# Graph attention layer on one core: node masks and counts made in the edge stage, part of the softmax work given to Pool, the last two adds of x given to DVE

## The reference

```python
h   = relu(layernorm(x))
msg = relu(h[src] + edge_attr);  p = msg @ W_fc.T + b_fc
scores = p @ Q.T                                   # one score for each head
w = exp(scores - segment_max(scores, dst)[dst])
alpha = w / max(segment_sum(w, dst)[dst], 1e-9)
pooled = [segment_sum(alpha[:, h:h+1] * p, dst) for each head]
mean_p = segment_sum(p, dst) / max(deg, 1)
gate = softmax(mean_p @ Wg.T + bg)                 # over the heads
out = x + sigmoid(sum_h gate[:, h] * pooled[h])
```

## Time and profile before

| | us |
|---|---|
| median of three runs (744.27 to 744.82) | 744.5 |
| the profiled execution | 740.5 |
| its span, from first to last instruction | 738.8 |
| DVE busy in the span | 487.2 |
| PE busy in the span | 553.3 |

### The profile page before, as it was taken

The page is one execution under the profiler, slowest core; times in us unless marked ns, Lnnn a source line. Parts: engine busy times, 40 slices in busy tenths (PEclk is TensorE's granted clock), DMA queues, the critical chain, the costliest instruction groups (busy, mean ns, idle before and its releaser), DMA issues.

```text
span 738.8 us, 12420 instructions
## 1 busy us (share of the span) xinstructions
PE 553.3 (75%) x2474; PEld 435.4 (59%) x2475; DVE 487.2 (66%) x1651; ACT 383.7 (52%) x661; POOL 440.3 (60%) x334
## 2 busy tenths in 40 slices
PE   3418988988889867989003998889888778877775
PEld 2206866766668656767002876777666666655554
DVE  4118677868679767878998766666565655554552
ACT  2105455646557455664130244666766575666663
POOL 7765556666651655640000256677878787778887
PEclk9999899989999999999655999999999999999998
DMA  7434455555553577775000799999999999999998
GB/s 222 136 92 145 142 163 172 169 167 171 169 173 117 162 230 254 242 256 188 25 0 3 251 361 366 307 305 324 358 327 340 335 345 316 320 332 343 336 340 277
DMA packets 137238, 171.53 MB, mean 232 GB/s; under 512 B 10096, under 2 KB 123784, under 8 KB 137202
## 3 DMA queue, kind: packets, MB, share of 16 engines
q10 hardware_dynamic: 91344, 90.23, 37.2%
q1 hardware_dynamic: 33010, 42.70, 18.2%
q0 software_dynamic: 12848, 38.20, 16.2%
HBM read 111.50 MB, written 59.60 MB: 232 GB/s over the span
## 4 chain that ended last, share of the span: by engine, by line
PE 46%; DVE 14%; issue 9%; ACT 8%; another core or an unknown queue 7%; POOL 6%; ACTq 4%; DMA 2%; DVEq 2%; POOLq 0%; SPq 0%
PE bank L726 23%; PE bank L809 16%; POOL arena L444 6%; PE bank L716 5%; ACT arena L583 5%; DVE spread L1196 3%; ACTq L586 2%; ACT bank L559 2%; DVE p_keep L997 1%; ACTq L538 1%; DVE stats L977 1%; DVEq L1200 1%; ACTq L591 1%; DMA p_keep<-in_x_dram,idx 1%
## 5 line engine op out<-in xcount | busy, mean ns | idle before, releaser
L809 PE MATMUL bank<-p_keep,spread 128*128 x1172 | 273.4, 387 | 54.4 <-DVE spread L1196 46.1
L444 POOL TENSOR_TENSOR arena<-arena 128x1024 f32<-128x1024 f32 x96 | 224.7, 2350 | 144.0 <-ACT arena L583 143.6
L809 PEld LDWEIGHTS bank<-p_keep,spread 128*128 128x128 f32 x1172 | 217.4, 191 | 111.2 <-issue 84.2
L1196 DVE TENSOR_SCALAR spread<-bank,rel,wgt 128x128 f32<-128x128 f32 x586 | 195.8, 403 | 130.9 <-PE bank L809 78.7
L726 PE MATMUL bank<-w_all,arena 128*128 128x264 f32 (+1 forms) x784 | 232.1, 423 | 43.2 <-ACT arena L491 22.3
L726 PEld LDWEIGHTS bank<-w_all,arena 128*128 128x128 f32 (+1 forms) x784 | 146.1, 207 | 68.7 <-ACT arena L491 36.3
L583 ACT ACTIVATE arena<-bank 128x1024 f32<-128x1024 f32 x97 | 99.2, 1022 | 144.8 <-PE bank L809 131.9
L431 POOL DMA_INDIRECT p_keep<-in_x_dram,idx x124 | 120.4, 971 | 71.6 <-issue 32.6
L491 ACT ACTIVATE arena<-bank 128x256 f32<-128x256 f32 x196 | 72.9, 373 | 103.9 <-remote 51.4
L431 POOL DMA_INDIRECT arena<-in_x_dram,idx x72 | 70.1, 974 | 60.8 <-ACT arena L483 33.9
L559 ACT ACTIVATE bank<-zero 128x1024 f32<-128x1024 f32 x98 | 100.5, 1026 | 3.0
(11 more groups left out here) (197 smaller groups left out, 163.7 us busy)
## 6 DMA issues: line engine op xcount, KB each, us to landing
out_dram<-arena ACTq DMA_DIRECT2D x97, 512.0 KB, 4.5
arena<-in_x_dram ACTq DMA_DIRECT2D x73, 512.0 KB, 5.4
arena<-in_edge_attr_dram SPq DMA_DIRECT2D x48, 512.0 KB
arena<-in_x_dram POOLq DMA_DIRECT2D x24, 512.0 KB, 5.7
p_spill<-p_keep SPq DMA_DIRECT2D x16, 512.0 KB
p_keep<-p_spill SPq DMA_DIRECT2D x16, 512.0 KB, 5.5
p_keep<-in_x_dram,idx POOLq DMA_INDIRECT x124
arena<-in_x_dram,idx POOLq DMA_INDIRECT x72
```

The source lines that it names most:

```text
L444: pool.tensor_tensor(yout[:, slot, :, :], yout[:, slot, :, :], xin[:, slot, :, :], ALU.add).then_inc(summed, 1)
L809: nc.tensor.matmul(places[:, bass.ds(place, T)], spread[:, k0 + k, :], p_rows[:, bass.ds(p_at, T)], start=False, stop=True, skip_group_che ...
L1196: v.tensor_scalar(spread[:, k, :], bank[:, 7, P:2 * P], rel[:, bass.ds(s0 + k, 1)], wgt[:, bass.ds(s0 + k, 1)], ALU.is_equal, ALU.mult).th ...
```

## The change

1. Masks and node counts, which DVE made at the head of the softmax stage, are made in the edge stage by a new function `node_work(k)`, one instruction at a time in iterations 60 to 100. The counts come from a forward scan and a backward scan with a maximum. From them `less` = -1/count is made there too, with two reciprocals of 128x128.
2. In the backward scans of the exponents `ALU.add` becomes `ALU.max`, so that the mask product L1099 over 128x2304 falls away. For the gate logits a product of 128x1024 with (next - 1) takes its place. The ninth scan of each kind (the count), `deg` and its reciprocal fall away.
3. PE signals the first two turned heads on their own, and the first scan waits for these alone.
4. POOL, idle in the softmax stage, takes the floor at 1e-9, two products, the two comparisons for `sel_1`, and the correction for the tile's first node (`by_first`), as three instructions over all heads. DVE keeps the correction for the last node.
5. Around the start of the scatter stage DVE loads its two first words ahead of the copy of the weights, PE no longer waits for `wgt_ready`, and waits for one matrix at a time in its first six steps.
6. At the end DVE, not POOL, adds x to groups 96 and 97.
7. The buffers move: masks to `spread`, `w_run` to `arena`, `keep_neg` to `w_all`.

```diff
+            def node_work(k):
+                b = k % 2
+                blk = slice(b * P, (b + 1) * P)
...
+                elif k in (78, 79):
+                    v.tensor_tensor_scan(in_first[:, blk], same[:, blk], ones[:, :], 0.0, ALU.mult, ALU.add
+                                         ).then_inc(node_step, 1)
+                elif k in (82, 83):
+                    dve.wait_ge(node_step, 12)
+                    v.tensor_tensor_scan(less[:, blk][:, ::-1], same_next[:, blk][:, ::-1], in_first[:, blk][:, ::-1], 0.0,
+                                         ALU.mult, ALU.max).then_inc(node_step, 1)
...
+                elif k in (88, 89):
+                    dve.wait_ge(node_step, 15)
+                    v.reciprocal(less[:, blk], less[:, blk]).then_inc(node_step, 1)
...
-            then(v.tensor_tensor(run, run, end.unsqueeze(1).broadcast_to([P, C, RW]), ALU.mult))
...
-            for n in range(C):
+            for n in range(K):
                 ins = v.tensor_tensor_scan(tot[:, n, ::-1], same_next[:, ::-1], run[:, n, ::-1], 0.0,
-                                           ALU.mult, ALU.add)
+                                           ALU.mult, ALU.max if n < H else ALU.add)
...
+            v.scalar_tensor_tensor(run[:, H:K, :], same_next.unsqueeze(1).broadcast_to([P, H, RW]), 1.0, run[:, H:K, :],
+                                   ALU.subtract, ALU.mult)
...
-            then(v.tensor_scalar(deg, tot[:, K, :], 1.0, None, ALU.max))
-            then(v.reciprocal(deg, deg))
-            then(v.tensor_tensor(run[:, 0:H, :], tot[:, H:K, :], over_h(deg), ALU.mult))
+            then(v.tensor_tensor(run[:, 0:H, :], tot[:, H:K, :], over_h(less), ALU.mult))
+            dve.sem_inc(mean_ready, 1)
...
+            sums = tot[:, 0:H, :]
+            pool.wait_ge(ends_ready, 2)
+            pool.tensor_scalar(sums, sums, 1e-9, None, ALU.max).then_inc(sums_ready, 1)
...
+            pool.wait_ge(gain_ready, 1)
...
+            pool.tensor_tensor(by_head(sums), by_head(w_run), gain_of, ALU.mult).then_inc(by_first_done, 1)
+            pool.wait_ge(by_first_done, 1)
+            pool.tensor_tensor(tot[:, 0:2, :], tot[:, 0:2, :], tot[:, 2:4, :], ALU.add).then_inc(by_first_done, 1)
+            pool.wait_ge(by_first_done, 2)
+            pool.tensor_tensor(tot[:, 0, :], tot[:, 0, :], tot[:, 1, :], ALU.add).then_inc(by_first_done, 1)
...
+            dve.wait_ge(by_first_done, 3)
+            then(v.copy_predicated(total, in_first.bitcast(I32), tot[:, 0, :]))
             dve.sem_inc(c_ready, 1)
```

More of the change, by code:

```diff
@@ L454, in _ @@
             add_four(FULL - FULL % 4 - 4, False, [k for k in BY_POOL if FULL - FULL % 4 + k < FULL])
[L455 to L473, removed]
         @block.scalar
@@ L786, in _ @@
             turn_chain(C, 2)
+            pe.wait_ge(selected, BLK)
             pe.wait_ge(c_ready, 1)
@@ L796, in _, with steps @@
             p_rows = p_keep[:, :, :].rearrange("p t d -> p (t d)")
-            def steps(half, s0, k0, n):
+            def steps(half, s0, k0, n, apart=3):
                 _, words = nc.values_load_multi_w_load_instructions(
@@ L810, in steps @@
                                      start=False, stop=True, skip_group_check=True).then_inc(stepped, 1)
-            pe.wait_ge(wgt_ready, 1)
             pe.wait_ge(words_in, 64)
             pe.sem_inc(stepped, AHEAD)
-            with pe.Fori(0, TURNS) as turn:
+            steps(0, 0, 0, HALF, 1)
+            steps(1, 0, HALF, HALF)
+            with pe.Fori(1, TURNS) as turn:
                 for h in range(2):
@@ L1076, in _ @@
             for n in range(H, K):
-                v.tensor_tensor_scan(run[:, n, :], same, row(n), 0.0, ALU.mult, ALU.add)
-            v.tensor_tensor_scan(run[:, K, :], same, tot[:, 0, :], 0.0, ALU.mult, ALU.add).then_inc(rows_read, 1)
-            v.tensor_scalar(cneg, cm, 1.0, BIG, ALU.subtract, ALU.mult)
-            v.tensor_scalar(wneg, one_node, 1.0, BIG, ALU.subtract, ALU.mult)
-            v.tensor_scalar(end, same_next, -1.0, 1.0, ALU.mult, ALU.add)
+                ins = v.tensor_tensor_scan(run[:, n, :], same, row(n), 0.0, ALU.mult, ALU.add)
+            ins.then_inc(rows_read, 1)
+            dve.wait_ge(rows_read, 1)
+            v.scalar_tensor_tensor(run[:, H:K, :], same_next.unsqueeze(1).broadcast_to([P, H, RW]), 1.0, run[:, H:K, :],
+                                   ALU.subtract, ALU.mult)
             def link(k, keeps, pad, ops, count):
@@ L1204, in _ @@
             dve.wait_ge(words_in, 64)
-            for h in range(2):
-                need(h)
-                spreads(0, h * HALF, HALF)
+            first, second = need_word(0), need_word(1)
+            dve.wait_ge(p_ready, first & 255)
+            dve.wait_ge(zeroed, first >> 8)
+            dve.wait_ge(wgt_summed, 1)
+            then(v.tensor_copy(wgt[:, 0:P], bank[:, 7, 2 * P:3 * P]))
+            dve.sem_inc(wgt_ready, 1)
+            spreads(0, 0, HALF)
+            dve.wait_ge(p_ready, second & 255)
+            dve.wait_ge(zeroed, second >> 8)
+            spreads(0, HALF, HALF)
             dve.wait_ge(wgt_summed, 2)
```

185 lines of the change are left out of this document (121 added, 64 removed).

## The result

The changed kernel takes 733.5 us (median of four runs, 728.5 to 734.6) against 744.4 for the kernel before, measured beside it: a ratio of 0.984, interval 0.981 to 0.988. That is 10.9 us faster by the medians and 9.2 to 14.4 by the interval; 6.6 was forecast. In two later groups of runs the two kernels stood at 740.7 and 730.7 us, 10.0 apart (0.989, interval 0.986 to 0.991, so 6.7 to 10.3 us), and at 664.7 and 656.4 us, 8.3 apart (0.987, interval 0.983 to 0.990, so 6.4 to 11.4 us). Medians are taken over the executions that are not over 1.5% above the fastest of their kernel.

A forecast was written before the change was run, and what follows sets the result against it. The prediction took the softmax stage as one chain on DVE and the scatter stage as paced by transfers. Savings 13.3 - 5.7 - 1.0 = 6.6 us gave 744.5 - 6.6 = 737.9 us, range 731.0 to 741.5.

The forecast's parts named there:

- The savings on DVE: Softmax stage: removed, shortened or moved instructions, and an earlier first scan (1.0 us), take 11.4 us off DVE.
- POOL's prices: Softmax stage: POOL's new instructions take 8.9 us together, all hidden behind DVE's own work if nothing disturbs.
- The meeting cost: Softmax stage: POOL and DVE take turns on operands in SBUF, instruction by instruction, which loses 5.7 us.
- The rival without a cost: Softmax stage: POOL and DVE run side by side, the sum is 12.3 us, time 732.2 us; chance 0.25.
- The edge stage: Iterations 60 to 100: about 6.1 us of added DVE work costs 1.0 us, between 0 and 4.6.
- The sign of failure: Edge stage: the prediction fails if this stage ends more than 4 us later.
- A whole upper bound in the edge stage: Rival: the masks cost the edge stage 4.6 us, leaving 3.0 us gained, 741.5 us; chance 0.12.
- a scatter stage that gives back half: Rival: transfers, rather than their start, set the scatter stage's end; half the gain returns, 741.2 us; chance 0.07.
- The loss through a lower clock: Rival, edge stage: all 6.1 us on PE's path, clock 0.84 adds 3.2 us; 746.2 us, slower than before; chance 0.06.
- The end: End of the span: DVE adding groups 96 and 97 saves 1.5 us, between 0.5 and 1.8.
- The start: Start of the scatter steps: loading the words first saves 0.4 us, between 0 and 1.3.
- the prediction's term of nothing for this stage: Scatter stage: paced by its transfers, its length stays; first step to last sigmoid within 1 us.

The follow-up runs named there:

- the probe: The changed kernel with POOL's softmax kinds of instruction run behind its last step, alone and beside DVE work, on tiles no longer needed; span 778.1 us.

## Why the prediction was right

The direction, the range and the mechanism held; the size was short by 4.3 us in the medians of the first runs, by 3.4 and 1.7 in the two later groups. By its own steps:

The bound. DVE's chain in the softmax stage did shorten the span by as much as it lost, and no new wait took its place.

The savings on DVE. 11.4 us were worked out. The run with nothing on POOL allows a check: 50.6 - 44.3 + 4.6 returned to DVE = 10.9. The largest miss is at the head, 0.7 instead of 1.0 (1.59 to 0.90 us), since the first four turned pieces reach DVE 0.85 us after PE's start rather than 0.51.

POOL's prices. For one-input work I took 1.2 and 0.75 us and the probe says 2.77 and 1.76, both above the upper bounds that I had set from rows of two-input work. All eight instructions together are 12.6 us alone, not 8.9. This did not matter to DVE's path, because the cover was large (9 and 7 us) and because one-input work stops DVE less.

The meeting cost. 5.7 us were taken; 10.9 - 7.0 = 3.9, or 10.9 - 6.5 = 4.4 in the other order, were lost, of which 0.3 are added waits. For the first five instructions 3.1 were taken and 2.3 were lost, for the last three 2.6 and 1.4 or 1.9. The walk let every POOL instruction cost its whole length: beside the comparisons DVE's products of two inputs (L1210, L1211) kept their 1.22 and 0.69 us, and POOL's large product in the correction lay under the reciprocal in the first profile (387.65 to 389.85). That the engines take turns is shown by the probe and by the short instructions without POOL. The rival without a cost (732.2 us) came nearer to the median of the first runs (733.5) than the forecast did, but its mechanism is refuted: the softmax stage would have fallen to 39.2 us, and it fell to 43.6. It is a case in which the time alone would have chosen the wrong explanation.

The edge stage. 1.0 us was taken, and 1.0 to 2.0 are measured where it can be measured. That the 4.8 us between the first two profiles were mostly the stage's own wandering is likely, not shown: ends with masks lay between 348.3 and 355.7 (seven profiles, mean 351.7), without between 348.5 and 350.8 (three, mean 349.4). The sign of failure that the prediction had named, an end more than 4 us later, came in the first pair of profiles and in neither of the other two, where the end moved by -2.5 (350.8 to 348.3) and 2.0 (271.9 to 273.9). The idle time of 15.8 us in which the masks were to hide was not all waiting for PE, as the prediction had it: the profile puts 8.8 us of it down to PE and 5.4 to a release that it can't name. The prices of the masks add up to 6.0, not 6.1, and the growth of PE's time at a clock of 0.84 is 3.3, not 3.2; neither moves the forecast.

The other rivals. A whole upper bound in the edge stage would have left 3.0 us, and a scatter stage that gives back half would have left 3.3; all three groups show more. The loss through a lower clock did not come: the granted clock from 140 to 205 us is 0.97 in the first two profiles of the changed kernel, and the 0.89 of the earlier trace rows was 0.97 in the next profile of before.

The end. 1.5 taken, 1.7 measured. The start: 0.4 taken, 0 to 0.6 left open.

Put together with the measured sizes: 6.5 to 7.0 (softmax) + 1.7 (end) + 0 to 0.6 (start) - 1.0 to 2.0 (masks) = 6.2 to 8.3 us. The last group gives 8.3 in the medians and 7.4 in its profiles (662.4 to 655.0). The other two give 10.9 and 10.0 in the medians, of which 1.7 to 4.7 us are not explained; by the intervals the second agrees with the sum (6.7 to 10.3), and the first, 9.2 to 14.4, does not. The remainder can only lie in the edge stage and the scatter stage. The scatter stage holds a hint. From the first step to the last sigmoid the kernel before takes 329.2, 328.9 and 329.3 us, the changed kernel 327.3, 328.5 and 328.2, and of the eight edited versions seven lie between 323.7 and 328.4 and one at 330.3. So the prediction's term of nothing for this stage may be short by about 1 us or more, of which the start is a part. Why is open, and it would need more profiles of both kernels. No run tested that this stage is paced by its transfers.

## What to carry to other kernels

Before giving work from DVE to POOL, look at the operands of what DVE does meanwhile: beside two inputs in SBUF or a fast one-input instruction there, POOL's two-input instruction takes DVE's time nearly in full, and 4.6 us of offload bought 0.2 to 0.7; ACT took the eight products of the correction, and no instruction of DVE grew. A single serial chain is best shortened by removing instructions or by moving them to an earlier stage in which their engine still waits now and then, which here turned 5.5 us into 1 to 2. And when a change is smaller than what the other stages wander by, judge it by the length of its own stage in the profile, not by the whole.

## What the runs showed that was not expected

POOL takes longer for one input than for two: 2.77 us for a maximum with a constant over 1024 columns, 2.34 for a product of two tiles; 1.76 for a comparison of 586 columns with a value for each partition.

Where two instructions on two engines start within 10 ns, either may hold the other, and the stage has two lengths, 0.5 us apart. In all eight profiles of the pair the starts are within 10 ns, DVE went first in five and POOL in three.

In the last group of runs the edge stage took 272 us, in all others about 350, with the same kernel. From 140 to 205 us its transfers moved 216 GB/s rather than 166, while the scatter stages took 324 to 330 us in all groups. The cause is open: the record gives the same chip number for the last group and for the one before it, so it is not shown to be a property of one chip.
